# A decoder block on one core: x transposed by DMA and normalised by GpSimd, one copy of h transposed, waits reordered

## The reference

```
x = x + attn(layernorm(x), W_qkv, W_out)             # causal, 16 heads of 16
x = x + cross(layernorm(x), ctx, mask)               # one head, softmax over 64 context tokens
x = x + ffn(layernorm(x), gate_w, down_w, norms)     # 704 inner features

def layernorm(x): return (x - mean(x)) / sqrt(var(x) + 1e-5)

def bit_linear(x, w, g):           # both products of the ffn
    xn = rms_norm(x, g)
    xq = round(xn * 127 / max|xn|) back by its scale    # per token
    wq = clip(round(w / mean|w|), -1, 1) * mean|w|
    return xq @ wq.T
y = bit_linear(x, gate_w, g1); gate, up = split(y); h = gate * sigmoid(gate) * up
return bit_linear(h, down_w, g2)
```

## Time and profile before

| | us |
|---|---|
| median of 3 runs | 209.47 (208.86 to 209.68) |
| the profiled run | 208.5 |
| its span | 206.5 |
| PE busy | 186.9 |
| DVE busy | 165.7 |
| ACT busy | 152.2 |
| POOL busy | 113.8 |

### The profile page before, as it was taken

The page is one execution under the profiler, slowest core; times in us unless marked ns, Lnnn a source line. Parts: engine busy times, 40 slices in busy tenths (PEclk is TensorE's granted clock), DMA queues, the critical chain, the costliest instruction groups (busy, mean ns, idle before and its releaser), DMA issues.

```text
span 206.5 us, 10407 instructions
## 1 busy us (share of the span) xinstructions
PE 186.9 (91%) x3967; PEld 149.6 (72%) x3967; DVE 165.7 (80%) x522; ACT 152.2 (74%) x438; POOL 113.8 (55%) x258
## 2 busy tenths in 40 slices
PE   3999999999998999999999999999999998885673
PEld 3878688977786778888787879788878776552341
DVE  1335599998895968988998889797979899999982
ACT  2378985858887686879878797977797877575651
POOL 6410328445746362665465575537483558787880
PEclk9999999999999999999999999999999999999999
DMA  5999100101002100020203000202001020300002
GB/s 169 383 342 354 58 3 3 54 3 52 3 0 86 51 3 25 0 78 2 76 0 103 28 29 2 76 2 73 3 26 52 20 63 27 103 5 2 25 25 76
DMA packets 11474, 12.82 MB, mean 62 GB/s; under 512 B 1010, under 2 KB 10674, under 8 KB 11444
## 3 DMA queue, kind: packets, MB, share of 16 engines
q1 hardware_dynamic: 11444, 12.46, 18.6%
HBM read 10.36 MB, written 2.10 MB: 60 GB/s over the span
## 4 chain that ended last, share of the span: by engine, by line
PE 73%; issue 8%; DVE 7%; ACT 7%; POOL 2%; DMA 1%; ACTq 1%; DVEq 0%; SPq 0%; POOLq 0%
PE ps L366 13%; PE ps L350 8%; PE ps L344 8%; PE ps L376 7%; PE ps L451 5%; PE ps L429 5%; PE ps L533 5%; PE ps L466 5%; PE ps L491 5%; PE ps L398 4%; PE ps L479 3%; PE ps L420 2%; PE ps L388 2%; PE ps L550 2%; DVE wg L1411 1%
## 5 line engine op out<-in xcount | busy, mean ns | idle before, releaser
L2006 POOL TENSOR_TENSOR zh<-hh,gd 128x352 f32<-128x352 f32 x32 | 29.9, 949 | 9.9 <-DVE hh L1350 9.6
L366 PE MATMUL ps<-yaT,wqk 128*128 128x128 f32 x256 | 31.9, 278 | 0.6 <-ACT yaT L701 0.5
L1925 POOL TENSOR_SCALAR ve<-mv 128x1 f32<-128x1 f32 x32 | 7.8, 243 | 42.9 <-issue 34.4
L366 PEld LDWEIGHTS ps<-yaT,wqk 128*128 128x128 f32 x256 | 30.2, 194 | 1.6 <-ACT yaT L701 1.2
L1222 DVE TENSOR_REDUCE mx<-ps 128x16 f32<-128x1024 f32 x16 | 19.6, 1224 | 10.2 <-PE ps L398 9.9
L350 PE MATMUL ps<-wg,zT 128*128 128x352 bf16 x128 | 22.7, 312 | 2.9 <-ACT hT L704 1.3
L805 ACT ACTIVATE th_sb<-ps,th 128x352 f32<-128x352 f32 x32 | 17.5, 552 | 6.5 <-PE ps L350 3.1
L1927 POOL TENSOR_TENSOR rs<-ve,neghalf 128x1 f32<-128x1 f32 x32 | 20.5, 641 | 2.7
L762 ACT ACTIVATE pT<-ps 128x512 f32<-128x512 f32 x32 | 17.8, 597 | 4.4 <-PE ps L436 4.3
L701 ACT ACTIVATE v<-ps 64x128 f32<-64x128 f32 x64 | 17.6, 274 | 2.8 <-PE ps L376 2.2
L350 PEld LDWEIGHTS ps<-wg,zT 128*128 128x128 bf16 x128 | 11.3, 97 | 9.9 <-issue 2.3
(11 more groups left out here) (117 smaller groups left out, 486.6 us busy)
## 6 DMA issues: line engine op xcount, KB each, us to landing
ct_in<-ctx_t SPq DMA_DIRECT2D x16, 128.0 KB, 2.2
cn_in<-ctx_n SPq DMA_DIRECT2D x16, 128.0 KB, 2.2
out<-o_out SPq DMA_DIRECT2D x16, 128.0 KB, 1.7
wg<-gate_t SPq DMA_DIRECT2D x1, 1408.0 KB, 8.2
x_in<-x SPq DMA_DIRECT2D x1, 1024.0 KB, 11.5
wd<-down_t SPq DMA_DIRECT2D x1, 640.0 KB, 8.9
wqk<-wqkv_t SPq DMA_DIRECT2D x1, 512.0 KB, 4.0
x_in<-x SPq DMA_DIRECT2D x1, 512.0 KB, 9.0
```

The source lines that it names most:

```text
L366: last = pe.matmul(qk_ps[:, e * P:(e + 1) * P], wqk[:, c, e * P:(e + 1) * P], yaT[:, t % 2, c, :], start=(c == 0), stop=(c == DC - 1))
L2006: G.tensor_tensor(zh[:, t % 2, part], hh[:, t % 2, part], gd[:, part], ALU.mult).then_inc(ev[f"zh_d{j}"], 1)
```

## The change

Seven things are changed.

1. **x transposed for tiles 4 to 15.** A transposed copy of x (`x_t`) is passed in and loaded by `load_xt` in two groups. The numbers of each token (rs1 and sh1), which lie one per partition, are stored in DRAM (`keep_norms`) and loaded back as rows onto all partitions (`spread_norms`). POOL computes yaT = x_t times one row (`scale_x`) plus the other (`shift_x`) for each tile. The transposes by PE, `normalise_x` and `keep_yaT` of these tiles are gone.
2. **Tile 0** is normalised by DVE (`normalise_first`) from mean and inverse root, without sh1.
3. **The products before the first tile** (to start PE) multiply zeros that DVE writes, 3 of 512 columns in place of 7 of 128 on the identity matrix, and don't wait for a load.
4. **One copy of h transposed**: all six pieces go to bank 0, and one ACT copy of 768 columns takes them.
5. **Waits on PE**: `freed(users)` now comes before the wait for the data.
6. **SP's list**: `load_xt(3)`, `keep_norms(3)`, `spread_norms(3)` and `load_xt(4)` stand before `load_ctx(0)`, and `keep_norms(4)`, `spread_norms(4)` before `load_ctx(1)`; stores and context loads are interleaved in a new way after that.
7. **The lists** of PE, ACT, DVE and POOL have a new order in many places, and the bank users named in them change accordingly. PE's idle-filling products (`keep_busy`) are 22 in place of 15.

The core of the diff:

```diff
-WARM = 7
+WARM = 3
+XF = 4
+        norm1_rows = nc.dram_tensor("norm1_rows", (2, T, P), F32, kind="Internal").ap()
+        xt_in = sb("xt_in", [P, T - XF, DC, P])
+        norm1_all = sb("norm1_all", [P, 2, T - XF, P])
-        hT_ps = [bank(0, 2 * P).bitcast(F16), bank(5, (IC - 4) * P // 2).bitcast(F16)]
+        hT_ps = bank(0, IC * P // 2).bitcast(F16)
+            def load_xt(k):
+                t0, t1 = groups[k]
+                sp.dma_start(xt_in[:, t0 - XF:t1 - XF, :, :], x_t[t0:t1, :, :, :].rearrange("t p c n -> p t c n")).then_inc(xt_ld[k], 16)
+            def keep_norms(k):
+                t0, t1 = groups[k]
+                sp.wait_ge(rstd1[k], 1)
+                sp.wait_ge(sh1_d[k], 1)
+                for a, part in enumerate((rs1, sh1)):
+                    with nc.allow_non_contiguous_dma(reason="one number of each token"):
+                        sp.dma_start(norm1_rows[a, t0:t1, :].rearrange("t p -> p t"), part[:, t0:t1]).then_inc(rows_st[k], 16)
+            def spread_norms(k):
+                t0, t1 = groups[k]
+                sp.wait_ge(rows_st[k], 32)
+                for a in range(2):
+                    sp.dma_start(norm1_all[:, a, t0 - XF:t1 - XF, :].rearrange("p t n -> p (t n)"),
+                                 norm1_rows[a:a + 1, t0:t1, :].rearrange("a t n -> a (t n)").broadcast_to([P, (t1 - t0) * P])).then_inc(rows_ld[k], 16)
             load_x(3)
             load_x(4)
+            load_xt(3)
+            keep_norms(3)
+            spread_norms(3)
+            load_xt(4)
             load_ctx(0)
+            keep_norms(4)
+            spread_norms(4)
             load_ctx(1)
             load_ctx(2)
             load_ctx(3)
...
+            def normalised(t):
+                if isinstance(t, int) and t < XF:
+                    pe.wait_ge(ev["yaT_d"], t + 1)
+                else:
+                    pe.wait_ge(ev["yaT_p"], at(t - (XF - 1)))
             def project_qk(t, *users):
-                pe.wait_ge(ev["yaT_d"], at(t + 1))
-                freed(users)
                 if first(t):
                     pe.wait_ge(wqk_in, 16)
+                freed(users)
+                normalised(t)
...
+            def transpose_h(t, *users):
                 if first(t):
                     pe.wait_ge(pads_set, 3)
+                freed(users)
                 pe.wait_ge(ev["hq_d"], at(t + 1))
+                transposes(hT_ps, hq_halves[:, t % 2, :, 0], IC, ev["hT_ps"], ident_16)
...
+            still = hq[:, 0, 0:P]
+            pe.wait_ge(still_set, 1)
+            for _ in range(WARM):
+                pe.matmul(ps[:, 7, :].rearrange("p (n k) -> p n k", k=P), still, still.unsqueeze(1).broadcast_to([P, 4, P]), start=True, stop=True)
             pe.wait_ge(cst_in, 16)
...
             def step(s):
+                scores_q(s, ("exp_d1", s), ("exp_d0", s))
+                readout(s - 1, ("out_d", s - 5))
                 transpose_z(s - 4)
-                scores_q(s, ("exp_d0", s), ("exp_d1", s))
-                readout(s - 1, ("out_d", s - 5))
                 cross_readout(s - 3)
-                transpose_ya(s + 1, ("zT_d", s - 3))
-                gate_up_1(s - 4, ("mx_d", s + 1))
-                gate_up_0(s - 4)
-                transpose_yx(s - 2, ("yaT_d", s + 2))
+                gate_up_0(s - 4, ("mx_d", s + 1))
+                gate_up_1(s - 4)
+                transpose_yx(s - 2)
                 transpose_readout(s - 1, ("x2_d", s - 2))
                 project_qk(s + 1)
                 cross_scores(s - 2, ("v_d", s + 1))
-                transpose_h_1(s - 5, ("h1_d1", s - 3))
-                transpose_h_0(s - 5)
                 transpose_max(s, ("h1_d0", s - 3))
                 project_out(s - 1)
-                scores_k(s, ("hT_d1", s - 4), ("hh_d0", s - 3), ("hh_d1", s - 3), ("mT_d", s + 1))
-                down(s - 5, ("k0_d", s + 2), ("k1_d", s + 2))
+                transpose_h(s - 5)
+                scores_k(s, ("hh_d0", s - 3), ("mT_d", s + 1), ("hh_d1", s - 3))
+                down(s - 5)
                 transpose_cross_weights(s - 2, ("x1_d", s))
                 project_v(s + 1)
...
+            def normalise_first():
+                dve.wait_ge(rstd1[0], 1)
+                V.tensor_scalar(ya[:, 0, :], x_in[:, 0, :], mv1[:, 0, 0:1], rs1[:, 0:1], ALU.subtract, ALU.mult).then_inc(ya_first, 1)
...
+            def rows(t, a):
+                return norm1_all[:, a, t - XF, :].unsqueeze(1).broadcast_to([P, DC, P])
+            def scale_x(t):
+                k, dst = x_ready(t)
+                pool.wait_ge(xt_ld[k], 16)
+                pool.wait_ge(rows_ld[k], 32)
+                after(pool, ev["qk_ps"], t - 1)
+                after(pool, ev["v_ps"], t - 1)
+                G.tensor_tensor(dst, xt_in[:, t - XF, :, :], rows(t, 0), ALU.mult).then_inc(ev["xr_d"], 1)
+            def shift_x(t):
+                k, dst = x_ready(t)
+                pool.wait_ge(ev["xr_d"], t - XF + 1)
+                G.tensor_tensor(dst, dst, rows(t, 1), ALU.add).then_inc(ev["yaT_p"], 1)
```

More of the change, by code:

```diff
@@ L1438, in _ @@
             residual_1(0)
-            stats_x1(0)
             maxima(2)
             weight_sums_inverse(1)
+            max_rest(2)
+            normalise_readout(1)
+            max_lo(2)
+            stats_x1(0)
             variance_x1(0)
-            max_rest(2)
-            max_lo(2)
-            normalise_readout(1)
             weight_scales()
@@ L1468, in _ @@
             cross_maxima(1)
+            residual_1(2)
             scale_zm(0)
-            residual_1(2)
+            cross_sums_inverse(1)
             scale_rz(0)
-            stats_x1(2)
-            scale_qz(0)
-            weight_sums_inverse(3)
-            round_z(0)
-            maxima(4)
-            cross_sums_inverse(1)
-            cross_guard(1)
+            scale_qz(0)
+            round_z(0)
+            cross_guard(1)
+            maxima(4)
+            weight_sums_inverse(3)
+            stats_x1(2)
+            max_rest(4)
             variance_x1(2)
@@ L1512, in _ @@
             gated_1(1)
             scale_qh(0)
-            variance_x2(2)
-            max_lo(5)
+            ffn_input(2)
+            inner_0(1)
             round_h(0)
-            gated_0(1)
-            ffn_input(2)
             inner_1(1)
+            cross_maxima(3)
+            residual_1(4)
             ffn_largest(2)
-            inner_0(1)
+            stats_x1(4)
             scale_zm(2)
-            cross_maxima(3)
+            cross_sums_inverse(3)
+            variance_x1(4)
             scale_rz(2)
-            residual_1(4)
+            residual_3(0)
@@ L1692, in _ @@
+            scale_qh(6)
+            round_h(6)
+            max_lo(11)
             variance_x2(8)
-            scale_qh(6)
-            gated_0(7)
-            round_h(6)
-            gated_1(7)
+            cross_maxima(9)
+            inner_0(7)
             ffn_input(8)
-            max_lo(11)
-            inner_1(7)
-            inner_0(7)
-            cross_maxima(9)
+            residual_1(10)
             ffn_largest(8)
             scale_zm(8)
-            residual_1(10)
+            cross_sums_inverse(9)
@@ L2164, in _ @@
-            set_mask(11)
-            rstd_x2(9)
-            norm_weights_0(8)
-            norm_weights_1(8)
+            scale_ek(8)
+            rstd_x2(9)
+            scale_x(14)
+            set_mask(11)
+            norm_weights_1(8)
+            norm_weights_0(8)
+            scale_fd(7)
+            rstd_x1(11)
             scale_th(9)
+            shift_x1(11)
             scale_ea(9)
-            rstd_x1(11)
-            shift_x1(11)
+            set_mask(12)
+            inner_rms(8)
@@ L2276 @@
         "x": x.reshape(tiles, P, D),
+        "x_t": np.ascontiguousarray(x.reshape(tiles, P, DC, P).transpose(0, 3, 2, 1)),
         "ctx_n": ctx.reshape(tiles, P, D),
```

1014 lines of the change are left out of this document (491 added, 523 removed).

## The result

The changed kernel takes 243.68 us (median of four runs, 242.74 to 245.98) against 209.17 of the kernel before on the same chip: a ratio of 1.1665, with a 95% interval of 1.1571 to 1.1759. The forecast was 207.5, 203.8 to 212.5. The profiled execution took 242.93 us with a span of 241.1.

A forecast was written before the change was run, and what follows sets the result against it. PE was taken to bound the steady step (10.63 of 10.90 us), DVE the tail. Start +1.5, steady -3.2 and tail -0.3 sum to -2.0, from a median of 209.47 to 207.5; range 203.8 to 212.5.

The forecast's parts named there:

- The price of a packet: Start: 4-byte store packets cost between nothing and 54 ns of an engine, 15 taken, so 1 and 2 us.
- The first rival: Start, round trip of the rows: 4-byte packets cost 54 ns, context 1 lands near 52; 215.6 us, chance 0.13 with partial forms.
- Who pays: Start: context loads stand behind the rows' round trips in SP's in-order queue; start +1.5 us net.
- Context late by 2 us: Start: context 0 lands at about 33.3 against a demand at 31.2, so PE stands 2 us.
- Steady, -3.2: Ten steady steps: less PE transposing, fewer stalls and half the first steps' start-up gaps gone; -3.2 us, bounds 0 and -5.9.
- under 8: Steady part, sign in the profile: ACT's busy time falls by 1.15 to 7.73 us a step.
- The second rival: Steady part: GpSimd's two new operations keep DVE out for their length, DVE 11.05 a step; 212.2 us, chance 0.12.
- Start, gained: Before the first projection: warm-up without a load and DVE normalising tile 0 gain 1.0 us (0 to 1.3).
- Tail, -0.3: After the steady steps: -0.3 us, bounds -1.5 to +1, with the larger last copy of h costing +0.2.

The follow-up runs named there:

- the fourth test of stores: No decoder: pairs of packed 4-column stores, in the change's layout or two tensors; 17.7 and 10.6 us with engines idle, 19.0 and 10.2 beside VectorE's operations.
- e1: Changed kernel with SP's order alone altered: both first contexts and x_t of tiles 8 to 15 loaded ahead of keep_norms(3); 239.82 us in one execution.
- e2: Kernel before plus only the four small stores of the rows, behind both context loads, waited for only at the very end; 226.93 us, ratio 1.078.
- e6: Changed kernel with only the stores' form altered: each partition's numbers together in DRAM, a tensor per group, read with a stride; 214.09 us, ratio 1.020.
- e12: Kernel before plus one 512 KB load of x_t of tiles 4 to 7 that nobody reads; 211.36 us, ratio 1.006.
- e11: Changed kernel with partition-wise rows, contexts 0 to 3 and scale_x(4), shift_x(4) early, x_t of tiles 4 to 7 behind the small stores; median 208.99 us.

## Why the prediction was wrong, step by step

**The price of a packet.** This step failed. It took "a price per packet" for granted and argued only over its size, 0 to 54 ns, so that the stores' packets would take 1 and 2 us, at most 3.5 and 6.9, and land with the last of them. The packets are quick (7.7 ns each in the fourth test of stores, where 15 was taken); the landing is not: there it comes some 16 us behind them. It doesn't follow their number (waits of 17 us for 2 KB and for 4 KB), and depends on how close together the numbers lie (1.4 against 7.5 us). The first rival, "the round trip", had the right place and direction; with its 54 ns it gave 215.6, off by 28 us, because its upper bound came from a row about large packets, and because packets were the wrong thing to price. No row of before held a small store at all: the honest bound was open to one side.

**Who pays.** The forecast let only SP's queue, and what stands in it, pay. e1 and e2 show two shares: 3 us of 34 by the queue's order, 17 by the stores' mere presence. The other 14 or so no run takes apart; GpSimd's wait for the rows, and PE's for GpSimd, are in them. That a transfer can stop engines that do not wait for it was in no rival.

**Context late by 2 us.** With the stores cheap (e6) it was late by 4.0. The mechanism was right, but the context took 7.1 us from issue to landing behind 1.5 MB, where 4.4 were reckoned. And beside the wait the clock falls, which the forecast left out: from 36 to 44 us PE is busy 6.97 at 0.50, up to 3.5 us of which the full clock would have saved.

**Steady, -3.2.** Measured -2.1, in the seven other kernels with the change -1.9 to -2.7. The parts: the new operations take 0.728 and 0.726 us, forecast 0.73; DVE rises by 0.16 a step, forecast 0.1 to 0.2; the one copy of h takes 0.811, forecast 0.82, against the earlier trace rows. PE's busy time falls by 1.55 in ten steps, where two transposes at 0.22 a tile should give 2.2, and its idle time from 2.95 to 2.42. So two terms were mis-sized: 0.15 of PE's work a tile went, not 0.22, and 0.05 of its stalls a step, not 0.07 with half of the gaps of the first steps besides. No run took these two apart further, and the profiles of the kernel before with stores or a load added (e2, e12) have ten steps of 110.44 and 111.03 against 110.68, so a few tenths are scatter. ACT was to fall by 1.15 a step to 7.73; it fell by 0.68 to 8.28 (82.76 for ten against 89.56), which the forecast's mark "under 8" misses. Here the sum of durations misled: before, ACT's rows add up to 179.8 us where the page counts 152.2 busy, for neighbours on an engine overlap. So an operation that goes frees less than its row says, and PE's two transposes may well be the same case. The second rival is out in the steady part: `wf` has a mean of 0.477 against 0.529 before.

```profile
L1285 DVE SCALAR_TENSOR_TENSOR wf<-x,mv,gg 128x256 f32<-128x256 f32 x16 | 7.6, 477 | 0.0
```

**Start, gained.** Forecast -1.0; the first projection ends at 9.11 (7.09 + 2.02) against 9.81: -0.7.

```profile
7.09 2.02 PE L407 MATMUL ps<-yaT,wqk 128*128 128x128 f32 x16 [0.63 <-ACT yaT L728]
```

**Tail, -0.3.** Measured +0.5, and +0.1 to +0.7 in the others: within its bounds, on the wrong side. But e2 and e12, which have the old lists, show +0.5 and +0.6 too, so this may be scatter. No run shows the -0.3 that the forecast took, nor what the order of the waits costs.

## What to carry to other kernels

Never price a kind of transfer that the trace doesn't hold from the rows of another kind: measure it alone first, which takes one small kernel. To send one number per partition to DRAM, keep each partition's numbers together (16 bytes and more landed in 1.4 us, 8 bytes in 3.0) and let the reader take the stride; here that was worth 30 us for 0.13 us an operation. And look at what a new transfer does to everybody: idle time of several engines that ends at once, with the releasers `issue` or `remote`, can be a sign of transfers that no semaphore names, the engines' code among them.

## What the runs showed of the hardware that was not expected

- 128 numbers of 4 bytes, one from each partition, land in 1.4 us if they lie 32 bytes or more apart in DRAM, in 2.2 at 16, 2.7 at 8, and in 6.8 to 7.5 side by side (16 of them in 1.3); 8 bytes a partition, side by side, take 3.0, 16 bytes 1.4.
- The packets of such a pair of stores (1056, 7.7 ns each) start within 2 us; the landing comes 16 us later.
- While such a store is under way, a load of 128 KB takes 7.3 to 8.2 us instead of 2.95, on another engine's queue too, and an engine without any wait stood for 2.14 us beside one pair and 4.92 beside another, beside two others not at all.
- Reading one of two inputs of a GpSimd operation on 128x256 with a stride of 16 or 32 bytes costs 0.86 us against 0.73.
- A load of 512 KB that nobody uses cost a kernel 0.6%, with PE standing 1.70 us on `issue` in its trace.

Open: by what mechanism closeness makes a small store slow, and why the change's layout adds to it; when a store that has not landed stops an engine and when not; why a piece of PE's code comes 2.5 us late in some executions whose loads are those of before. Of the kernels tried, e11 has the lowest median, 208.99 against 209.47 of before, which is no difference that these runs can tell.
